# Two-layer attention and mixture-of-experts kernel: where the first layer's expert splits stand, and which engine issues the loads of the pairs' lines

## The reference

```python
def layer0_ffn(x):                       # 16 experts, 4 per token, F = 176, plus a shared one
    probs = softmax(x @ gate.T)
    top_vals, top_idx = top_k(probs, 4)
    dense_w = zeros(T, 16).at[arange(T)[:, None], top_idx].add(top_vals)
    g, u = einsum('th,ehf->tef', x, w_gate), einsum('th,ehf->tef', x, w_up)
    routed = einsum('te,tef,efh->th', dense_w, silu(g) * u, w_down)
    return routed + silu(x @ ws_gate) * (x @ ws_up) @ ws_down

xn = layernorm(x)
x = x + attention0(xn) + layer0_ffn(xn)  # one head of 256
xn = layernorm(x)
x = x + attention1(xn) + layer1_ffn(xn)  # 32 heads in 8 groups; 7 experts, 3 per token, F = 256
```

## Time and profile before

| | |
|---|---|
| median of 3 runs (lowest, highest) | 1134.88 us (1134.79, 1135.94) |
| the profiled execution: its time | 1137.65 us |
| its span, first to last instruction | 1135.8 us |
| TensorE matmul busy | 1015.3 us, 89% of the span |
| VectorE, ScalarE, GpSimd busy | 758.1, 592.0, 317.3 us |
| mean granted clock of TensorE | 0.957 of full speed |

### The profile page before, as it was taken

One profiled execution on the slowest core, in us unless ns is written; L12 is line 12 of the kernel. 1 busy time (PEld: TensorE's weight loads), 2 busy tenths in 40 slices (PEclk: granted clock), 3 DMA queues, 4 the chain that ended last, 5 costly groups with the idle time before them and its releaser, 6 DMA issues.

```text
span 1135.8 us, 17286 instructions
## 1 busy us (share of the span) xinstructions
PE 1015.3 (89%) x5701; PEld 744.4 (66%) x5701; DVE 758.1 (67%) x1575; ACT 592.0 (52%) x894; POOL 317.3 (28%) x330
## 2 busy tenths in 40 slices
PE   4999897769999927799998999999999987999996
PEld 3877776669999913555554555555555565888885
DVE  6576544465665436799889888888888846443438
ACT  6324544265555542466665666566656565444431
POOL 2005777065664410000000122222221000455342
PEclk9999999789999969799999999999999998999998
DMA  6862333354444272021121222222222115333244
GB/s 232 326 263 114 112 118 123 104 185 136 132 127 136 98 309 45 7 34 29 26 31 25 44 53 59 58 59 49 64 56 43 63 48 175 107 100 108 89 164 179
DMA packets 48962, 120.20 MB, mean 106 GB/s; under 512 B 7736, under 2 KB 24760, under 8 KB 48344
## 3 DMA queue, kind: packets, MB, share of 16 engines
q1 hardware_dynamic: 35968, 82.67, 25.3%
q0 software_dynamic: 11760, 32.24, 7.5%
q10 hardware_dynamic: 1152, 4.19, 0.9%
HBM read 72.17 MB, written 52.29 MB: 110 GB/s over the span
## 4 chain that ended last, share of the span: by engine, by line
PE 66%; DVE 14%; POOL 7%; ACT 4%; issue 4%; DMA 4%; SPq 0%; ACTq 0%; DVEq 0%; POOLq 0%
PE psum L827 10%; PE psum L849 10%; PE psum L836 8%; POOL xg L475 5%; PE psum L642 5%; PE psum L643 4%; PE psum L644 4%; DVE work_f L1726 4%; PE psum L556 4%; PE psum L557 3%; PE psum L558 3%; PE psum L628 3%; PE psum L653 2%; DVE x L1326 1%; ACT work_f L1219 1%
## 5 line engine op out<-in xcount | busy, mean ns | idle before, releaser
L1726 DVE TENSOR_REDUCE work_f<-psum 128x1 f32<-128x512 f32 x512 | 334.7, 684 | 51.0 <-PE psum L827 49.5
L1219 ACT ACTIVATE work_f<-psum 128x1024 f32<-128x1024 f32 x172 | 168.9, 1023 | 111.9 <-PE psum L836 108.6
L827 PE MATMUL psum<-work_r 128*128 128x512 f32 x512 | 205.0, 439 | 19.9 <-DVE work_f L1726 6.8
L482 POOL DMA_INDIRECT yk<-yb,dest x133 | 129.9, 977 | 241.9 <-ACT yb L1072 213.1
L827 PEld LDWEIGHTS psum<-work_r 128*128 128x128 f32 x512 | 94.2, 190 | 131.3 <-DVE work_f L1726 75.2
L836 PE MATMUL psum<-qm,work_r 128*128 128x512 f32 x512 | 161.9, 398 | 4.2 <-ACT work_f L1219 2.7
L475 POOL DMA_INDIRECT xg<-xn,slot x112 | 108.1, 966 | 180.4 <-PE psum L865 152.2
L836 PEld LDWEIGHTS psum<-qm,work_r 128*128 128x128 f32 x512 | 93.6, 188 | 31.8 <-ACT work_f L1219 10.9
L1219 ACT ACTIVATE pt<-psum 128x1024 f32<-128x1024 f32 x84 | 82.8, 1023 | 50.2 <-PE psum L836 47.6
L642 PE MATMUL psum<-wexp,xbh 128*128 x266 | 103.0, 387 | 6.5 <-issue 5.4
L643 PE MATMUL psum<-wexp,xbh 128*128 x266 | 96.9, 364 | 0.0
(11 more groups left out here) (218 smaller groups left out, 2044.7 us busy)
## 6 DMA issues: line engine op xcount, KB each, us to landing
xb<-xg SPq DMA_DIRECT2D x66, 258.0 KB
xg<-in_pad SPq DMA_DIRECT2D x1, 10320.0 KB
yg<-yk SPq DMA_DIRECT2D x20, 512.0 KB, 9.5
stage<-in_moe SPq DMA_DIRECT2D x16, 608.0 KB
xg<-in_pad SPq DMA_DIRECT2D x1, 7224.0 KB
work_r<-work_r SPq DMA_DIRECT2D x128, 48.0 KB
work_r<-work_r SPq DMA_DIRECT2D x32, 192.0 KB
stage<-in_moe SPq DMA_DIRECT2D x16, 384.0 KB, 3.8
```

The lines of the kernel that those rows point to most:

```text
L482: nc.gpsimd.indirect_dma_start(yk[l], bass.IndirectOffsetOnAxis(ap=dest[:, j % 8, i:i + 1], axis=0), yb[l][:, j % 2, i, :], None).then_inc ...
L827: nc.tensor.matmul(next_bank(pe, ("scores", n), b_mx, n + 1), qs[g % 2][:, t * P:(t + 1) * P], km[g % 4][:, r, :], start=True, stop=True). ...
L1219: nc.scalar.activation(pt[((b * NG + g) * QT + t) % 3][:, 2 * h:2 * h + 2, :], psum[:, 3 + 2 * h:5 + 2 * h, :], ACT.Exp, scale=float(HD) * ...
L1726: v.reduce_max(mx[:, s % 2, i:i + 1], ring["scores", n], AX.X).then_inc(b_mx, 1)
```

## The change

The high parts of expert 7 move on ScalarE from the middle of the last attention batch to behind its context copies, and those of expert 8 are put with them; the low part of expert 7 moves on VectorE behind the last addition to `x`. Of experts 9 to 15, ScalarE makes two behind pair 0 and one behind each of pairs 1 to 5 (before: two behind each of pairs 1 to 4). Experts 10 and 13 change places between GpSimd and VectorE. The loads of the lines of pairs 2 and up leave SP's stream in both layers: ScalarE issues them, pair `j + 3` right after the high parts of pair `j + 1`. SP keeps the first two pairs, and its expert loads follow one another with nothing between.

```diff
-        BY_DVE = (5, 6, 7, 8, 10, 12, 14, 15)
+        BY_DVE = (5, 6, 7, 8, 12, 13, 14, 15)
...
+        def pair_rows(l, j):
+            return xg[l][j * 2 * P:(j * 2 + blocks_of(l, j)) * P, :].rearrange("(n p) h -> p n h", p=P)
...
-            def load_pair(l, j):
-                if j >= 2:
-                    sp.wait_ge(m_tx, pairs(l, j - 1))
-                    sp.wait_ge(m_ix, pairs(l, j - 1))
...
+            def load_first_pairs(l):
+                for j in range(2):
+                    sp.dma_start(xb[l][:, j], pair_rows(l, j)).then_inc(m_xb[j], 16)
...
-            for e in range(8):
+            for e in range(9):
                 load_expert(e)
             sp.wait_ge(m_scat, scattered(0, 16 * TT * TOP0))
-            load_pair(0, 0)
-            load_pair(0, 1)
-            for e in range(8, 11):
+            load_first_pairs(0)
+            for e in range(9, E0):
                 load_expert(e)
-            more = {3: (11,), 4: (12,), 5: (13, 14), 6: (15,)}
-            for j in range(2, NPAIR[0]):
-                load_pair(0, j)
-                for e in more.get(j, ()):
-                    load_expert(e)
...
             low_expert(9)
-            more = {0: (11,), 1: (13,)}
+            low_expert(10)
+            more = {0: (11,)}
...
+            def load_pair(l, j):
+                act.wait_ge(m_ix, pairs(l, j - 1))
+                act.dma_start(xb[l][:, j % 2, 0:blocks_of(l, j)], pair_rows(l, j)).then_inc(m_xb[j % 2], 16)
+
             def routed(l, weights):
                 pair_high(l, 0)
+                load_pair(l, 2)
                 for j in range(NPAIR[l] + 2):
                     if j + 1 < NPAIR[l]:
                         pair_high(l, j + 1)
+                        if j + 3 < NPAIR[l]:
+                            load_pair(l, j + 3)
...
                 if not last:
                     projections(b + 1, 4)
-                else:
-                    high_expert(7)
...
             attention0(B - 1, True)
+            high_expert(7)
+            high_expert(8)
...
             def more_experts(j):
-                for e in {1: (8, 9), 2: (10, 11), 3: (12, 13), 4: (14, 15)}.get(j, ()):
+                for e in {0: (9, 10), 1: (11,), 2: (12,), 3: (13,), 4: (14,), 5: (15,)}.get(j, ()):
                     high_expert(e)
...
                     low_expert(6)
-                    low_expert(7)
...
             attention0(B - 1, True)
+            low_expert(7)
...
             def more_experts(j):
-                for e in {1: (8,), 2: (10,), 3: (12,), 4: (14, 15)}.get(j, ()):
+                for e in {0: (8,), 3: (12,), 4: (13,), 5: (14,), 6: (15,)}.get(j, ()):
                     low_expert(e)
```

23 lines of the change are left out of this document (7 added, 16 removed).

## The result

The changed kernel takes 1119.63 us (median of 4 runs, 1118.09 to 1122.68); the kernel before, on the same chip, 1134.84 (median of 4). The ratio is 0.9874, with a 95% interval of 0.9857 to 0.9891: 15.2 us faster by the medians, where 11.0 were forecast.

A forecast was written before the change was run, and what follows sets the result against it. TensorE's own time bounds the steady loop; about 16 us are lost in the first eight pairs. Pair 7 from 262.26 to 250.7 gives 11.6, less 0.6 is 11.0: median 1134.88 to 1123.9 us, range 1120.5 to 1130.5.

The forecast's parts named there:

- 0.6 for stretching: Whole sum: VectorE subtractions stretching, as one did to 1.72 us instead of about 1.0, would take 0.6 us off the gain.
- Contexts begin at 197.8 instead of 201.01. That is 3.2 us won.: End of attention: with expert 7's high part away from the `p_hi` copies, contexts follow the transposes sooner, 3.2 us won.
- Its 1.4 us are lost whole.: Ahead of pair 0: expert 7's low part on VectorE stands before the first `pair_low`, costing 1.4 us.
- Nothing on the path: First two pairs' lines, behind expert 8's load on SP: under 1 us later but needed 10 us later, so no cost.
- Pairs 2 and 3: Pair 2 begins at 226.6 against 226.26; pair 3, its lines in time, at 231.5 against 235.71, 4.2 us won.
- What was won is spent: At pair 2: splits 9 and 10 behind pair 0 use up the earlier gain; it begins at 226.6 against 226.26.
- Pairs 4 to 7: First layer: pairs 4, 5, 6 and 7 begin at 235.6, 240.3, 245.3 and 250.7; pair 7 waits for expert 15's low part.
- 4.5 us later: Pair 4's lines, issued by ScalarE at 224.1, are there 4.5 us later, at 228.6, in time.
- Issues hidden, the steady loop unchanged: Steady loop: ScalarE's issue of 0.36 us is hidden in 1.6 us idle per pair; pairs stay at 4.0 us.
- The wait for `m_ix` I cost at nothing: ScalarE, ahead of the issue: no cost, since VectorE takes a pair's targets before that pair's `pair_low`.
- The clock: Rival at pair 2: TensorE's clock falls to 1.2 GHz between two 1.1 us gaps; gain 8.6, 1126.3 us; chance 0.16.
- The rival of late lines: Pair 4's lines: transfers, not issue order, hold them, so pair 3 begins at 236.0; gain 6.5, 1128.4 us; chance 0.10.

The follow-up runs named there:

- the second profile of before: The kernel before run and profiled once more, nothing changed: median 1134.53 us, ratio 1.0008; the profiled execution took 1131.95 us.
- the second profile: The changed kernel run and profiled once more, nothing changed: median 1119.16 us, ratio 0.987 to the kernel before.
- the splits alone: The changed kernel with line loads issued by SP again in both layers, one expert load behind each of pairs 3 to 7's: 1117.53 us, ratio 0.985.
- buffer free earlier: The kernel before with GpSimd making expert 4's low part four scatters earlier, freeing the buffer of expert 7's load: 1128.61 us, ratio 0.9954.
- expert 7 alone: The kernel before with only expert 7's high part moved behind the context copies and its low part behind the last addition: 1123.39 us, ratio 0.9911.
- the doubled issues: The changed kernel with every pair load issued as two halves of 64 partitions: 1120.58 us, ratio 0.9879 to the kernel before.
- the version with early splits: The changed kernel with high parts of 9 and 10 before the first silu, low parts of 8 (VectorE) and 11 (GpSimd) earlier: 1115.51 us, ratio 0.9838.
- the issue alone: The kernel before with only pair-load issues moved to ScalarE, SP loading experts 8 to 15 consecutively, every split unchanged: 1130.04 us, ratio 0.9969.
- the version without GpSimd's subtractions: The version with early splits, plus low parts of 9 and 10 on VectorE and a one-column silu ahead of expert 9's high part: 1114.97 us, ratio 0.9825.

## Why the prediction was right in the sum and wrong in its terms

Against the second profile of before, the changed kernel's first one gains 11.1 us up to the contexts (200.84 to 189.72), gives back 1.7 from there to pair 0 (16.27 to 17.99), gains 3.9 from pair 0 to pair 7 (40.23 to 36.33) and 0.5 behind it: 13.8 of span, between two executions. The forecast had 3.2, -1.4 and 9.8, less 0.6 for stretching. That the sum came near is luck.

- **"Contexts begin at 197.8 instead of 201.01. That is 3.2 us won."** The step that failed. The mechanism was right, contexts now begin 1.40 us behind the transposes' work as forecast; the size was the remainder of a wait in one execution. The step took the transposes' 192.91 as given, while the row beside it, ScalarE's 4.32 us for expert 7's load, said that the contexts were tied to a load, not to TensorE. What that load waited for was not followed back. It leads to GpSimd, and then the wait is a difference of two streams, one of which varied by 7 us.
- **"Its 1.4 us are lost whole."** Right. From the start of the last addition to the first `pair_low`, VectorE takes 3.35 us (201.78 to 205.13), against 1.94 in the second profile of before (212.59 to 214.53): 1.4 of the 1.7 given back. By the same rows only 0.5 would have come back without that low part, since the late lines held the high part until 204.65.
- **"Nothing on the path"**, of the lines behind expert 8's load: wrong as soon as the contexts came 11 us earlier. TensorE waited 1.55 us for them, 1.86 in the second profile. It cost nothing measurable, since VectorE stands behind it.
- **Pairs 2 and 3.** Forecast 10.0 and 14.9 us behind pair 0, measured 9.93 and 14.86, with ScalarE's wait for expert 11 as forecast. "What was won is spent" is right from pair 0 to 2. At pair 3 the number is partly luck: the forecast has its `pair_low` end last, but that ended at 220.64, and TensorE reached the transposes of pair 4 only at 221.30, without a wait, from its own work.
- **Pairs 4 to 7.** Forecast 34.1 us from pair 0 to 7, measured 36.33 and 38.36 in two executions. From pair 3 to 4 alone it is 5.97 where 4.1 were forecast. The prediction's own sign of being wrong is there, gaps that end at `xb`: at the transposes of pair 5 and pair 7 (0.55 and 0.22; 1.53 at pair 7 in the second profile). The term that was too small is the "4.5 us later": pair 5's lines were issued 12.3 us behind pair 0, which the forecast's order gives too (its fourth `pair_high` ends at 12.5), but took 6.93 us to pair 5's transposes, with an expert load issued 0.03 us ahead of them:

```profile
219.97 0.33 SPq L341 DMA_DIRECT2D stage<-in_moe  x1
```

Behind such a wait the time ahead of the first matmul shows as well (0.95 and 1.09 us in the first profile), which can otherwise be hidden: pair 5's matmuls follow pair 6's transposes at once, 232.25 to 232.60. That this makes up the 2.2 us missing here is not shown: the splits alone, without such a gap behind pair 0, take 36.43. Pair 7 waits for expert 15's low part in both, as forecast. The other 3.7 of the missing 5.9 us come from the baseline: the 43.89 of the earlier trace rows are 40.23 in the second profile of before, where pair 6 takes 4.02 us and not 6.29, and 40.54 and 42.22 in the two other kernels with the old pairs (buffer free earlier, expert 7 alone).

- **Issues hidden, the steady loop unchanged:** right (25.00 of 25 us; the doubled issues).
- **"The wait for `m_ix` I cost at nothing":** ScalarE stood 0.60 us for it at pair 2 of the changed kernel, and 2.31 in the version with early splits, most of which it would have stood for TensorE anyway.
- **The rivals.** The clock did not fall at pair 2: its first matmul takes 0.42 us, and the window from 225 us on is at 1.00. The rival of late lines rested on a rule of the Trainium skill (DMA: Bandwidth & Descriptors, "Issuing engines are not separate DMA queues"): a second issuer saves only issuing time. The runs agree with it in their way: with the new splits, SP's issue is as good as ScalarE's. That the issue alone won 3.6 us with the old splits is no transfer made faster, but a line load that no longer stands behind another load's wait.

The two errors had opposite signs, 8 too few and 6 too many. The first and most of the second came from reading one execution's waits as the kernel's.

## What to carry to other kernels

A wait in a profile is the difference of two arrivals in one execution. Before its length is used as a gain, follow both sides back to what sets their time: if the late side hangs on an engine that waits for nothing (here GpSimd, by a buffer), the early side may be early by much more in the next execution, and a second profile of the kernel before costs little against that. Where two edits remove the same wait, their prices do not add (3.6 us alone, nothing on top); price the second with the first in place, and look for what ends within a microsecond behind the wait that goes.

## What the runs showed of the hardware

VectorE's small instructions took as long as GpSimd's large subtraction beside them. Timelines of VectorE and GpSimd in the changed kernel:

```profile
217.66 2.31 DVE L1487 COPY share<-xb 128x2 f32<-128x2 f32 x1
...
217.68 2.26 POOL L480 TENSOR_TENSOR wexp<-stage,wexp 128x960 fp32r<-128x960 f32 x1
...
226.50 2.09 DVE L1634 TENSOR_TENSOR wexp<-stage,wexp 128x256 fp32r<-128x256 f32 x1
...
226.07 2.24 POOL L480 TENSOR_TENSOR wexp<-stage,wexp 128x960 fp32r<-128x960 f32 x1
```

The copy of 128x2, 0.16 us elsewhere, ends at 219.97, and GpSimd's subtraction at 219.94; the subtraction of 128x256, 0.42 elsewhere, ends at 228.59, GpSimd's at 228.31. By these ends VectorE does not run slower, it stands until the other is done; a `pair_low`, with one input in PSUM, takes its usual 0.69 us beside GpSimd's subtraction (215.18, GpSimd from 214.78 to 217.03). The Trainium skill has it (SBUF — State Buffer, "Who interferes with whom"): VectorE's copies and casts in a two-port mode, and its instructions with two inputs in SBUF, contend with GpSimd for one shared pair of ports, and whoever issues first has it for the whole instruction while the other is blocked. The traces agree, the version without GpSimd's subtractions too; in which mode the copies ran no row shows. Whether the 1.72 us of the earlier trace rows, from which the prediction took its 0.6 for "stretching", are the same is not shown: GpSimd ran no subtraction when that instruction began. A low part on GpSimd costs the pairs not only its own 3 us, but whatever small copy of VectorE falls beside it.

ScalarE's issues run ahead of its computation: in the changed kernel the issue of pair 6's lines is at 222.47, while an expert's high part runs (222.22 to 223.21), and 1.05 us before the `pair_high` at 223.52 that stands ahead of it in the code. So ScalarE's stream is in order for its waits, but an issue can pass computation that is still queued. This fits with 2 x 0.62 us of issues per pair that lengthen neither the steady loop nor the silu's wait; no run here tests it by itself.
